# Query halves by column group in the weighted sum, and empty rows by a per-row scale and an eight-row product

## What is computed

```python
def gat_layer(x, graph, W, b):
    h = x @ W
    s = jnp.einsum('bnd,bmd->bnm', h, h) * graph
    s = jnp.where(s == 0.0, NEG_INF, s)          # NEG_INF = -1e+16
    a = jax.nn.softmax(s, axis=2)
    return jnp.einsum('bnm,bmd->bnd', a, h) + b
heads = jax.vmap(lambda W, b: gat_layer(flow_x, graph, W, b))(Wh, bh)   # 8 heads, 64 -> 128
x = jax.nn.leaky_relu(cat, negative_slope=0.01)                         # cat: 8 x 128 features
out = gat_layer(x, graph, W_out, b_out)                                 # 1024 -> 64
```

## Time and profile before

| | us |
|---|---|
| median of 3 runs | 2781.16 (2780.2 to 2785.39) |
| the profiled execution, its own time | 2786.11 |
| its span | 2784.3 |
| PE busy (and its weight loads) | 2259.4 (1463.7) |
| DVE busy | 2234.9 |
| ACT busy | 1471.3 |
| POOL busy | 602.4 |
| the hid stage | from about 963 to about 2477 |

### The profile page before, as it was taken

The page is one execution under the profiler, slowest core; times in us unless marked ns, Lnnn a source line. Parts: engine busy times, 40 slices in busy tenths (PEclk is TensorE's granted clock), DMA queues, the critical chain, the costliest instruction groups (busy, mean ns, idle before and its releaser), DMA issues. The chain is left out here.

```text
span 2784.3 us, 57963 instructions
## 1 busy us (share of the span) xinstructions
PE 2259.4 (81%) x24510; PEld 1463.7 (53%) x24510; DVE 2234.9 (80%) x2971; ACT 1471.3 (53%) x2331; POOL 602.4 (22%) x351
## 2 busy tenths in 40 slices
PE   3855556667767689999999898998998989968997
PEld 2632234444446555565555555655555556636665
DVE  6569985678874598988988989989889898837775
ACT  2412221369962156566566665665656656636665
POOL 0036662000000012222222222222222222210000
PEclk8968788879988779999999999999999999979999
DMA  2000000000000201010010010100100100010000
GB/s 104 1 0 0 0 0 0 2 1 1 1 2 1 59 23 39 17 47 25 24 40 25 27 38 17 48 25 25 40 25 28 36 17 32 25 47 1 1 1 31
DMA packets 61879, 60.79 MB, mean 22 GB/s; under 512 B 50368, under 2 KB 51520, under 8 KB 60992
## 3 DMA queue, kind: packets, MB, share of 16 engines
q1 hardware_dynamic: 61632, 57.21, 6.6%
HBM read 44.34 MB, written 4.46 MB: 18 GB/s over the span
## 5 line engine op out<-in xcount | busy, mean ns | idle before, releaser
L547 DVE CUSTOM_DVE_ANT_0 x_sb<-ps_score,hid_mask 128x1024 f32<-128x1024 f32 x512 | 616.5, 1204 | 142.4 <-PE ps_score L419 140.3
L628 ACT ACTIVATE x_sb<-x_sb,hid_neg_max 128x1024 f32<-128x1024 f32 x512 | 586.8, 1147 | 268.2 <-DVE hid_neg_max L547 268.1
L556 DVE STREAM_TRANSPOSE hid_weights_t<-x_sb 128x1024 f32<-128x1024 f32 x512 | 631.4, 1233 | 1.3 <-ACT x_sb L628 0.6
L419 PE MATMUL ps_score<-hid_y_hi,hid_xs 128*128 128x512 f32 x1024 | 471.4, 460 | 51.3 <-DVE hid_neg_max L547 47.8
L437 PE MATMUL ps_low<-hid_weights_t,hid_x_rep 32*64 32x256 f32 x16384 | 506.7, 380 | 0.8 <-ACT hid_share L656 0.8
L437 PEld LDWEIGHTS ps_low<-hid_weights_t,hid_x_rep 32*64 32x64 f32 x16384 | 346.2, 131 | 139.9 <-issue 82.3
L419 PE MATMUL ps_score<-hid_y_lo,hid_xs 128*128 128x512 f32 x1024 | 411.2, 402 | 0.0
L697 POOL TENSOR_TENSOR hid_z<-hid_z,hid_inv_cols 128x1024 f32<-128x1024 f32 x64 | 197.9, 3092 | 761.1 <-ACT hid_z L636 761.1
L419 PEld LDWEIGHTS ps_score<-hid_y_hi,hid_xs 128*128 128x128 f32 x1024 | 195.6, 191 | 257.5 <-issue 116.0
L690 POOL TENSOR_TENSOR hid_y_lo<-hid_y_wide,hid_y_hi 128x1024 fp32r<-128x1024 f32 x64 | 153.1, 2392 | 348.5 <-ACT hid_y_wide L623 348.5
L419 PEld LDWEIGHTS ps_score<-hid_y_lo,hid_xs 128*128 128x128 f32 x1024 | 197.1, 192 | 42.9 <-issue 14.6
(11 more groups left out here) (308 smaller groups left out, 3810.5 us busy)
## 6 DMA issues: line engine op xcount, KB each, us to landing
hid_inv_cols<-hid_inv_rows SPq DMA_DIRECT2D x64, 512.0 KB, 3.7
hid_x_rep<-h_sb SPq DMA_DIRECT2D x128, 64.0 KB, 2.5
adj_rows<-in_adj SPq DMA_DIRECT2D x8, 512.0 KB, 8.0
x_sb<-in_x SPq DMA_DIRECT2D x2, 1024.0 KB, 6.1
x_saved<-x_sb SPq DMA_DIRECT2D x1, 2048.0 KB, 6.5
x_sb<-x_saved SPq DMA_DIRECT2D x1, 2048.0 KB, 8.0
out_x<-x_sb SPq DMA_DIRECT2D x1, 2048.0 KB, 6.3
hid_inv_rows<-hid_row_inv SPq DMA_DIRECT2D x64, 4.0 KB, 1.4
```

Source lines behind the costliest of these rows:

```text
L419: ins = pe.matmul(m.ps_score[:, i % 2, half * HALF:(half + 1) * HALF], xs[:, g // HEADS % 2, t * P:(t + 1) * P], y[g % 2][k][:, half * HAL ...
L547: dve.tensor_tensor_reduce(ring[:, i % RING, :], m.ps_score[:, i % 2, :], mask[:, t, :], -1.0, HUGE, ALU.add, ALU.min, neg_max[:, g % 2, t ...
L556: dve.transpose(weights_t[:, g % 2, :, t, :], ring[:, i % RING, :].rearrange("p (b j) -> p b j", j=Q)).then_inc(tile_turned, 1)
L628: act.activation(ring[:, i % RING, :], ring[:, i % RING, :], ACT.Exp, scale=-1.0, bias=neg_max[:, g % 2, t:t + 1], accum_out=row_sum[:, g ...
```

## The change

Part one: in `values`, column group c takes a half of the queries (tiles 0 to 3, or 4 to 7) and all key blocks: 64 products of 128 columns in a quarter for 32 of 256. z has 512 columns for 1024, with one query half in each half of the partitions, and is complete. `copy_z` and `normalise` run over half of the columns, `inv_cols` is filled by two DMAs. `head_out` takes 64 rows of weights and z for each half of the queries, and `project_out` does so for `wx`.

Part two: a block `empty_rows`, once, behind the layer norm: it finds the empty rows of all batches, the rows that have at least one neighbour that isn't empty (by a product with the graph), `row_scale` (-1 or 0 for each row and batch) and `zero_cols` (8 x 1024, one row for each batch). `mask_tile` uses the graph's mask with `row_scale` in the place of -1.0; `project` adds a third product to each half, `pick_batch` (8 x 128, `ZERO_COL` in the batch's row) by `zero_cols`, of 8 rows. The mask of a batch, its sums and tests and their waits are gone. The layer norm's block has the weights' loads no more: they are issued at the start of the hid stage, whose first work is now to turn the rows, with fold and gram behind.

```diff
+def empty_rows(nc, m):
...
+        @block.vector
+        def _(dve):
+            for q in range(4):
+                ins = dve.tensor_reduce(top[:, 2 * q:2 * q + 2, :], m.h[:, 2 * q:2 * q + 2, :, :], AX, ALU.max)
+            ins.then_inc(found, 1)
+            dve.wait_ge(found, 1)
+            dve.tensor_scalar(lives[:], top[:], 0.0, None, ALU.is_gt).then_inc(ready, 1)
+            dve.tensor_scalar(zero[:], top[:], 0.0, None, ALU.is_le).then_inc(ready, 1)
+            dve.tensor_scalar(sign[:], top[:], 0.0, -1.0, ALU.is_gt, ALU.mult).then_inc(found, 1)
+            dve.wait_ge(found, 2)
+            dve.wait_ge(counted, 1)
+            dve.scalar_tensor_tensor(out=m.row_scale[:], in0=m.ps_score[:, 0, 0:NT * B]
+                                     .rearrange("p (t b) -> p t b", b=B), scalar=0.0,
+                                     in1=sign[:], op0=ALU.is_gt, op1=ALU.mult)
+            dve.wait_ge(turned, 1)
+            dve.tensor_copy(m.zero_cols[:], m.ps_score[0:B, 1, :])
+        @block.tensor
+        def _(pe):
+            pe.wait_ge(ready, 1)
+            for t in range(NT):
+                for j in range(NT):
+                    ins = pe.matmul(m.ps_score[:, 0, t * B:(t + 1) * B], m.adj_t[:, j, t * P:(t + 1) * P],
+                                    lives[:, j, :], start=(j == 0), stop=(j == NT - 1))
+            ins.then_inc(counted, 1)
+            pe.wait_ge(ready, 2)
+            for t in range(NT):
+                ins = pe.matmul(m.ps_score[0:B, 1, t * P:(t + 1) * P], zero[:, t, :], m.ident[:],
+                                start=True, stop=True)
...
             def project(g):
                 for half in range(2):
                     for k in range(2):
-                        ins = pe.matmul(m.ps_low[:, y_banks(g) + half, :], gram[k][:, g % HEADS, :],
-                                        xs[:, g // HEADS % 2, half * HALF:(half + 1) * HALF],
-                                        start=(k == 0), stop=(k == 1))
+                        pe.matmul(m.ps_low[:, y_banks(g) + half, :], gram[k][:, g % HEADS, :],
+                                  xs[:, g // HEADS % 2, half * HALF:(half + 1) * HALF],
+                                  start=(k == 0), stop=False)
+                    ins = pe.matmul(m.ps_low[:, y_banks(g) + half, :], m.pick_batch[:, g // HEADS, :],
+                                    m.zero_cols[:, half * HALF:(half + 1) * HALF],
+                                    start=False, stop=True)
...
                 for b in range(part * NB // 4, (part + 1) * NB // 4):
-                    c = b % 2
                     for a in range(P // Q):
-                        ins = pe.matmul(m.ps_low[c * F:(c + 1) * F, a, 0:NT * Q],
-                                        x_rep[a * Q:(a + 1) * Q, g // HEADS % 2, b, :],
-                                        weights_t[a * Q:(a + 1) * Q, g % 2, b, :, :],
-                                        start=(b == c), stop=(b == NB - 2 + c))
+                        for c in range(2):
+                            ins = pe.matmul(m.ps_low[c * F:(c + 1) * F, a, 0:NT // 2 * Q],
+                                            x_rep[a * Q:(a + 1) * Q, g // HEADS % 2, b, :],
+                                            weights_t[a * Q:(a + 1) * Q, g % 2, b,
+                                                      c * NT // 2:(c + 1) * NT // 2, :],
+                                            start=(b == 0), stop=(b == NB - 1))
...
             def head_out(g):
                 pe.wait_ge(z_normed, g + 1)
                 for half in range(2):
-                    ins = pe.matmul(m.ps_low[:, half, :], wz[:, g % HEADS, :],
-                                    z[:, half * HALF:(half + 1) * HALF], start=True, stop=True)
+                    rows = slice(half * F, (half + 1) * F)
+                    ins = pe.matmul(m.ps_low[:, half, :], wz[rows, g % HEADS, :], z[rows, :],
+                                    start=True, stop=True)
                 ins.then_inc(hidden_ready, 1)
...
+                for half in range(2):
+                    pe.matmul(m.ps_low[half * F:(half + 1) * F, 0, :], wo[:, g % HEADS, :],
+                              hidden[:, half * HALF:(half + 1) * HALF], start=True, stop=False)
+                for half in range(2):
+                    rows = slice(half * F, (half + 1) * F)
+                    ins = pe.matmul(m.ps_low[rows, 0, :], wx[rows, g % HEADS, :], z[rows, :],
+                                    start=False, stop=True)
...
-                dve.tensor_tensor_reduce(ring[:, i % RING, :], m.ps_score[:, i % 2, :], mask[:, t, :],
-                                         -1.0, HUGE, ALU.add, ALU.min,
+                dve.tensor_tensor_reduce(ring[:, i % RING, :], m.ps_score[:, i % 2, :], m.mask[:, t, :],
+                                         m.row_scale[:, t, g // HEADS:g // HEADS + 1], HUGE,
+                                         ALU.add, ALU.min,
                                          neg_max[:, g % 2, t:t + 1]).then_inc(masked_ready, 1)
...
-                    if n < B and u == HEADS - 1:
-                        build_mask(n, t)
...
-                act.copy(z[:].rearrange("p (t a j) -> p a t j", t=NT, a=P // Q),
-                         m.ps_low[:, :, 0:NT * Q].rearrange("p a (t j) -> p a t j", j=Q)).then_inc(z_ready, 1)
+                act.copy(z[:].rearrange("p (t a j) -> p a t j", t=NT // 2, a=P // Q),
+                         m.ps_low[:, :, 0:NT // 2 * Q].rearrange("p a (t j) -> p a t j", j=Q))\
+                   .then_inc(z_ready, 1)
```

More of the change, by code:

```diff
@@ L21 @@
 EPS = 1.0e-5
+ZERO_COL = -2.0 ** 100
 class Chain:
@@ L367, in load_rows @@
                         sp.dma_start(dst, m.h[q * Q:(q + 1) * Q, :, n, :]).then_inc(rows_loaded, 16)
+            for place, src in w.loads:
+                sp.dma_start(place, src).then_inc(weights_loaded, 16)
             sp.dma_start(x_saved, m.x[:].rearrange("p t b f -> p (t b f)")).then_inc(x_copied, 16)
@@ L452, in project_out @@
                 pe.wait_ge(hidden_done, g + 1)
[L453 to L464 removed]
+                for half in range(2):
[5 more added lines that the diff above has]
+                                    start=False, stop=True)
+                ins.then_inc(out_ready, 1)
+            for part in range(2):
+                turn_rows(0, part)
+            pe.wait_ge(weights_loaded, 16 * len(w.loads))
             for h in range(HEADS):
@@ L473, in _ @@
             ins.then_inc(folded, 1)
+            pe.wait_ge(x_split, 2)
+            for h in range(HEADS):
+                if h > 1:
+                    pe.wait_ge(gram_split, h - 1)
+                w2 = wh_t[:, h, :, :].rearrange("p a f -> p (a f)")
+                pe.matmul(m.ps_low[:, h % 2, 0:P], w2, w2, start=True, stop=True).then_inc(gram_ready, 1)
             pe.wait_ge(gram_split, HEADS)
-            for part in range(2):
-                turn_rows(0, part)
-            pe.wait_ge(ones_ready, 2)
             pe.wait_ge(fold_taken, 3)
-            for half in range(2):
-                sum_cols(0, half)
-            pe.wait_ge(zeros_ready, 2)
             project(0)
@@ L562, in invert @@
                 dve.reciprocal(row_inv[:, g % 2, :], row_sum[:, g % 2, :]).then_inc(inv_ready, 1)
-            dve.memset(hidden[:, 0:P], 1.0).then_inc(ones_ready, 1)
-            dve.wait_ge(ones_ready, 1)
-            dve.tensor_copy(ones[:], hidden[:, 0:P]).then_inc(ones_ready, 1)
-            for h in range(HEADS):
-                dve.wait_ge(gram_hi, h + 1)
-                dve.tensor_tensor(gram[1][:, h, :], m.ps_low[:, h % 2, 0:P], gram[0][:, h, :],
-                                  ALU.subtract).then_inc(gram_split, 1)
+            split_rows(0, 0)
+            split_rows(0, 1)
+            dve.wait_ge(weights_loaded, 16 * len(w.loads))
             dve.tensor_scalar(bias_pos[:], bias[:], 0.99, None, ALU.mult).then_inc(fold_taken, 1)
@@ L2117, in four_layers @@
                         layer(nc, m, g)
+            with fresh_semaphores(nc), ExitStack() as own:
+                layer_norm(nc, m, "ln3", Weights(nc, own, "ln3"))
+                empty_rows(nc, m)
         if stages is None or 3 in stages:
```

113 lines of the change are left out of this document (42 added, 71 removed).

## The result

The changed kernel takes 2944.19 us (median of 4 runs, 2939.93 to 2945.59) against 2783.27 for the kernel before in the same comparison: ratio 1.0573, 95% interval 1.0556 to 1.059. It is 161 us slower; the forecast was no change, 2781, with a range up to 2830.

The account below looks back on a forecast made before the run. PE was taken to set the attention stage's pace, except for DVE's mask bursts. Terms -69 + 43 + 5 - 6 + 25 + 2 = 0 gave 2786 us on the profiled execution, 2781 against the median; range 2745 to 2830.

Parts of the forecast that it names:

- Part 3: Values in query halves: eight 128-column records run side by side at 0.109 each, 1.75 a part for 1.73; +5 us.
- the -6 at the stage's end: End of the attention stage: halved copy_z, normalise and head output, for two head outputs standing alone in a row; -6 us.
- Rival 2: Values: PE can't take in twice the records; at 25 ns a record +67 us, 2848 us; chance 0.13.
- Part 2: Eight-row products added to the projection in 62 units, with their changes of shape: 0.70 each, +43 us (+12 to +70).
- the reserve: ACT's slack ahead of the activation: rounding could come 0.43 us later at no cost, if normalise were faster.
- The 0.15 for the output projection: Output projection: a second shape for its last two products costs one more way between shapes, 0.15 us a unit.
- Part 1: Masks of a batch removed from DVE: 7 batches at 12.0, less 15 for turning rows that stays; -69 us.
- the 12.0 a batch: Attention units where DVE makes the next batch's mask: 185.30 us for eight, 12.0 more than eight plain units.
- Part 4 and 5: The once-run block of empty rows, +25 us, and the stage's start with the weights' loads uncovered, +2 us (-2 to +5).

Follow-up runs that it names:

- e1: The changed kernel with the weighted sum of the kernel before put back, so the empty-rows part alone; 2772.35 us, ratio 0.9953.
- e5: e1 without the eight-row products, so that empty columns stay unmasked; 2743.43 us, ratio 0.9856.
- e3: Kernel before, products of values cut in two in 28 of 32 key blocks, both halves in a row on the same PE tile; 2971.97 us, ratio 1.0669.
- e12: e7 with the eight minima of a batch placed in tiles where POOL is idle, over two units; 2732.78 us, ratio 0.9815.
- e7: Kernel before with empty rows by a per-row scale and the batch's mask by a plain bf16 minimum, no eight-row product; 2769.67 us, ratio 0.9942.

## Why the prediction was wrong

**Part 3, query halves, is the step that failed:** "Eight side by side at that pitch: 16 x 0.109 = 1.75. Term: 256 x 0.02 = +5". It measured +134 alone and +172 with the other part. I took the time of a record on PE's array from a row of 16 records, where no supply of instructions can show, and never asked what 33,000 more instructions need to reach PE. In PE's timeline, e1 against the changed kernel, the tiles with values take 699.3 and 852.6 us in all, so 153 of the 172 lie there: 256 x 0.10 = 26 is the smooth lengthening of a tile (3.14 for 3.04), and some 125 is PE waiting for packets. Another 62 x 0.15 = 9 is the output projection with its second shape; some 10 aren't placed. What Part 3 says of copy_z and normalise was right (0.59 and 1.56 us after; normalise 3.09 before), but that was off the path; of the -6 at the stage's end some 2 came, an estimate from the time behind the last reciprocal (326.0 for 324.3) and the last unit's values (14.8 for 11.3).

Rival 2 had the place, the sign, and the test ("values still 3.04 per tile: 3.3 would be rival 2"), but its mechanism was a floor for each record, with +67. The Trainium skill, "TensorE: Matmul & The Clock Gate", section "Wait — 56ns, not 53.3ns?", has a floor near 25 ns from start to start. It doesn't show here, where the records fall on different row and column groups: 128 of a tile start within some 1.85 us, 14 ns each, as long as the packets are there. The average need was in the prediction (23 ns a record), and so was the idea of evening out; what was missing is that the evening-out has to be made by a supply with a rate of its own. Its chance, 0.13, was too small, and the range stopped below its price.

**Part 2** went as described but smaller. In e1 rounding comes 0.83 later (forecast 0.98), the reserve eats 0.44 of it, as read, and the chain grows by 0.39 a unit where I had 0.55. The normalise needn't be halved for that: in e1 it isn't. The shape change costs 0.09 each way here; I had taken 0.39 a round trip from values, and why it is more there wasn't tested. The 0.15 for the output projection came as forecast, but isn't in e1, which has the old one. From the first of its four products to the next of another kind it takes 1514.80 to 1516.66 in e1 and, in the changed kernel,

```profile
2347.98 1.08 PE L504 MATMUL ps_low<-hid_hidden,hid_wo 128*64 128x512 f32 x4 [0.85 <-ACT hid_hidden L657]
2348.99 1.08 PE L508 MATMUL ps_low<-hid_z,hid_wx 64*64 64x512 f32 x4
2350.00 0.50 PE L467 MATMUL ps_score<-hid_y_hi,hid_xs 128*128 128x512 f32 x1
```

2.02, for 1.86. So the term is 62 x 0.54 = 33 for 43 us.

**Part 1**, -69: with e5, which has neither masks nor eight-row products, the kernel is 37 us under before, and 25 us of start are in it, so -62 by the medians; from the first to the last reciprocal the profiled executions have 1372.4 for 1441.0, -69, as forecast. The scale by pointer (1269 for 1204 ns) is inside. One reading was off: the 11.74 us of the earlier trace rows, taken as eight masks alone, hold one of 3.36 us beside POOL's split; without POOL one mask comes every 1.2 us. How much of the 12.0 a batch was POOL's part wasn't asked. **Part 4 and 5**, +27: 25 measured, at the forecast clock of 0.50. The 64 products took 13.8 (forecast 13.6), the eight of `ident` 3.6 (3.7), the reductions 4.6 (4.97):

```profile
962.90 4.60 DVE L301 TENSOR_REDUCE empty_top<-h_sb 128x16 f32<-128x1024 f32 x4 [0.30 <-PEq L53]
...
967.78 13.81 PE L320 MATMUL ps_score<-empty_lives,adj_t_sb 128*128 128x8 f32 x64 [27.73 <-DVE empty_lives L304]
981.53 3.58 PE L325 MATMUL ps_score<-ident,empty_zero 128*8 128x128 f32 x16
...
995.93 3.68 PE L516 MATMUL ps_low<-hid_wo,hid_weights_t 128*128 128x64 f32 x16 [5.22 <-DMA hid_bias<-in_bh_t]
```

The last line is the lost cover of the weights' loads: 5.22 us of PE waiting for a DMA, a little over the 2 to 5 given. Without part 3 and the 9 for the output projection the sum was -8 on the kernel before, and e1 shows -13.

## What to carry to other kernels

A product with fewer rows wasn't cheaper where it changed the shape between two large ones; padded with zeros it saved 23 to 26 us. And before work is taken off an engine with a costly substitute, see whether it only stood at a bad place: masks made by a simpler instruction while POOL was idle left the batch's last units no longer than plain ones (21.66, 21.84 and 21.49 against 21.64).

## What was unexpected of the hardware

- Packets of PE's instruction queue (16 KB, 256 instructions) never follow in less than 3.23 us in any trace of this case, though one takes 1.1 us; PE's holes end 2.2 to 3.0 us after a packet's start.
- Two products in a row on the same tile of PE: 128 records in 2.82 us (e3), 2.09 when eight tiles take turns (changed kernel).
- bf16 minimum of two tiles 128x1024 on DVE: 680 to 691 ns in e12, where POOL is idle, and up to 3319 ns beside POOL's work in e7.
